# A vision tower on one core: the attention peaks turned into rows by four heads in three parts, in place of six heads in two

## What is computed

```python
qkv = x_qkv.reshape(B, N, 3, NUM_HEADS, HEAD_DIM).transpose(2, 0, 3, 1, 4)
attn = jax.nn.softmax(jnp.einsum('bhqd,bhkd->bhqk', q, k) * scale, axis=-1)
x_attn = jnp.einsum('bhqk,bhkd->bhqd', attn, v)
y2 = jnp.concatenate([x_mlp, x_attn], axis=-1)
```

## Time and profile before

| | us |
|---|---|
| median of 3 runs | 1977.3 |
| lowest, highest | 1976.71, 1978.36 |
| the profiled execution | 1970.27 |
| its span | 1968.5 |

### The profile page before, as it was taken

How to read it: one execution, slowest core, us unless ns; L and a number is a source line. 1 busy time by engine, 2 the same in 40 slices (tenths; PEclk the granted TensorE clock), 3 DMA queues, 4 the chain that set the end, 5 groups by cost and what they waited for, 6 DMA issues and landing times.

```text
span 1968.5 us, 38799 instructions
## 1 busy us (share of the span) xinstructions
PE 1608.9 (82%) x12434; PEld 1287.7 (65%) x12434; DVE 1226.8 (62%) x2822; ACT 845.9 (43%) x1934; POOL 248.9 (13%) x318
## 2 busy tenths in 40 slices
PE   4116289978898799987899789987899788998998
PEld 2004177757686577766777577765787577777786
DVE  2466757684686747685676837776576847563553
ACT  1001065434544345434554345433554346445653
POOL 2002101110022001110021100210011100210000
PEclk8557589978899779987999789987999789999999
DMA  2896646445555435555355446446364442212220
GB/s 72 221 229 163 172 83 143 109 111 132 122 122 113 119 87 137 136 117 136 95 114 134 108 101 149 111 114 159 69 145 116 109 121 50 39 23 41 51 56 15
DMA packets 161084, 218.51 MB, mean 111 GB/s; under 512 B 135099, under 2 KB 149605, under 8 KB 150118
## 3 DMA queue, kind: packets, MB, share of 16 engines
q10 hardware_dynamic: 12288, 154.15, 29.7%
q1 hardware_dynamic: 148582, 61.68, 17.8%
HBM read 186.57 MB, written 28.90 MB: 109 GB/s over the span
## 4 chain that ended last, share of the span: by engine, by line
PE 39%; issue 37%; DMA 9%; DVE 8%; POOL 3%; ACT 2%; SPq 1%; POOLq 0%; DVEq 0%; ACTq 0%
PE bank L952 7%; PE bank L859 7%; DMA xt<-in_x_dram 4%; PE bank L887 4%; PE bank L921 3%; PE bank L869 3%; DMA ks<-qk_scratch 3%; PE bank L906 2%; DVE psums L1211 2%; POOL var L1466 2%; PE bank L767 2%; PE bank L783 2%; DVE peaks L1403 2%; PE bank L734 1%; PE bank L849 1%
## 5 line engine op out<-in xcount | busy, mean ns | idle before, releaser
L1403 DVE TENSOR_REDUCE peaks<-bank 98x2 f32<-98x392 f32 x768 | 425.4, 562 | 318.6 <-PE bank L887 301.3
L1099 ACT ACTIVATE Pb<-bank 98x392 f32<-98x392 f32 x768 | 374.8, 497 | 337.5 <-PE bank L906 285.6
L1211 DVE TENSOR_REDUCE psums<-xt 112x2 f32<-112x512 f32 x672 | 442.6, 679 | 85.1 <-DMA xt<-in_x_dram 52.3
L887 PE MATMUL bank<-ks,qs 96*98 96x196 f16 x1536 | 274.1, 267 | 62.9 <-DVE peaks L1403 40.3
L952 PE MATMUL bank<-w2T,hid 128*98 128x192 f32 x1536 | 306.2, 338 | 0.0
L906 PE MATMUL bank<-qs,ks 97*98 97x196 f16 x1536 | 275.0, 264 | 3.1 <-ACT Pb L1099 2.7
L887 PEld LDWEIGHTS bank<-ks,qs 96*98 96x98 f16 x1536 | 164.8, 130 | 171.7 <-issue 79.5
L952 PEld LDWEIGHTS bank<-w2T,hid 128*98 128x98 f32 x1536 | 244.7, 173 | 2.6
L921 PE MATMUL bank<-Pb,vals 98*32 98x196 f32 x3072 | 186.7, 365 | 5.1 <-DVEq L1397 2.5
L906 PEld LDWEIGHTS bank<-qs,ks 97*98 97x98 f16 x1536 | 173.8, 134 | 17.4 <-issue 9.6
L734 PE MATMUL bank<-spread_p,cst 112*24 112x196 f32 x192 | 49.2, 406 | 127.0 <-POOL spread_p L1457 127.0
(11 more groups left out here) (181 smaller groups left out, 1896.6 us busy)
## 6 DMA issues: line engine op xcount, KB each, us to landing
xt<-in_x_dram ACTq DMA_DIRECT2D x96, 1568.0 KB, 9.1
qk_scratch<-qk SPq DMA_DIRECT2D x64, 294.0 KB, 3.7
qs<-qk_scratch SPq DMA_DIRECT2D x192, 73.5 KB, 3.3
ks<-qk_scratch SPq DMA_DIRECT2D x192, 73.5 KB, 3.6
out_dram<-fin SPq DMA_DIRECT2D x64, 147.0 KB
qs<-shiftT SPq DMA_DIRECT2D x128, 2.3 KB
hid<-in_L_ffn_w_dram SPq DMA_DIRECT2D x1, 1440.0 KB
hid<-in_L_ffn_w_dram SPq DMA_DIRECT2D x1, 960.0 KB
```

Of the source, the lines that this page charges most:

```text
L887: mm = pe.matmul(peak_ps[s][0:HT, T * q:T * q + T], qs[0:KS, i % NSTACK, h, HT * q:HT * q + HT], ks[0:KS, i % NSTACK, h, :], start=True, s ...
L1099: act.activation(Pb[:, (H * i + h) % NP, :, :].rearrange("p a b -> p (a b)"), score_ps[s][0:HT, 0:2 * T], ACT.Exp, scale=float(DH) ** -0.5 ...
L1211: last = dve.tensor_reduce(psums[:, m % 2, t, 2 * p:2 * p + 2], v[:, 2 * p:2 * p + 2, :, :], AX.XY, ALU.add)
L1403: dve.tensor_reduce(peaks[:, h // 6, :, h % 6], peak_ps[s][0:HT, 0:2 * T].rearrange("p (q k) -> p q k", q=2), AX.X, ALU.max, negate=True). ...
```

## The change

The peaks become rows in three parts of four heads (QUAD = 4) in place of two parts of six. `peaks` and `shiftT` have the shapes that go with it, there are three `shift_in` semaphores, and scores wait at heads 0, 4 and 8. Parts 0 and 1 of image i + 1 now follow the mixes in slots 5 and 9 of image i. Part 2 of image i follows the mix in slot 1 of image i itself, so it stands behind that slot's `fill`, which holds `project`. In `opening`, parts 0 and 1 of image 0 come at i = 4 and i = 6; part 2 is in slot 1 of the turn that follows.

```diff
-        if i == 4:
-            ops.append(("shift", dg, 0, 0))
-    ops.append(("shift", dg, 0, 1))
+        if i in (4, 6):
+            ops.append(("shift", dg, 0, i // 2 - 2))
...
         if i:
-            fill[0] = [("shift", 0, i, 1)] + fill[0]
...
         if i + 1 < GRP:
-            fill[7] = [("shift", 0, i + 1, 0)] + fill[7]
             fill[10] = [("values", 0, i + 1)] + fill[10]
...
             ops += fill[h]
             if h in (MIX_LAG, QUAD + MIX_LAG):
                 ops.append(("mix", 0, i, h // QUAD - 1))
-            if i and h == MIX_LAG - 4:
-                ops.append(("mix", 0, i - 1, H // QUAD - 1))
+                if i + 1 < GRP:
+                    ops.append(("shift", 0, i + 1, h // QUAD - 1))
+            if h == MIX_LAG - QUAD:
+                if i:
+                    ops.append(("mix", 0, i - 1, H // QUAD - 1))
+                ops.append(("shift", 0, i, H // QUAD - 1))
...
-        peaks = sb("peaks", [HT, 2, 2, 6])
-        shiftT = sb("shiftT", [6, 2, T], F16)
+        peaks = sb("peaks", [HT, H // QUAD, 2, QUAD])
+        shiftT = sb("shiftT", [QUAD, H // QUAD, T], F16)
...
-                sp.wait_ge(shift_ready, 2 * n_ + part + 1)
-                sp.dma_start(qs[KS:KS + 1, i % NSTACK, 6 * part:6 * part + 6, :],
+                sp.wait_ge(shift_ready, H // QUAD * n_ + part + 1)
+                sp.dma_start(qs[KS:KS + 1, i % NSTACK, QUAD * part:QUAD * part + QUAD, :],
                              shiftT[:, part, :]).then_inc(shift_in[part], 16)
...
-                if h % 6 == 0:
-                    pe.wait_ge(shift_in[h // 6], 16 * (GRP * G_ + i + 1) + ONE)
+                if h % QUAD == 0:
+                    pe.wait_ge(shift_in[h // QUAD], 16 * (GRP * G_ + i + 1) + ONE)
...
-                if h % 6 == 5:
+                if h % QUAD == QUAD - 1:
                     dve.wait_ge(peak_free[s], n_ + ONE)
                     dve.sem_inc(peaks_ready, 1)
```

More of the change, by code:

```diff
@@ L515, in bass_vit_tower @@
         shift_ready = sem("shift_ready")
-        shift_in = [sem(f"shift_in{s}") for s in range(2)]
+        shift_in = [sem(f"shift_in{s}") for s in range(H // QUAD)]
         oT_ready = sem("oT_ready")
@@ L893, in shift @@
                 ps, full = ring(at, "shift", (dg, i, part))
-                pe.wait_ge(peaks_ready, 2 * (GRP * G_ + i) + part + 1)
+                pe.wait_ge(peaks_ready, H // QUAD * (GRP * G_ + i) + part + 1)
                 for q in range(2):
-                    mm = pe.transpose(ps[0:6, HT * q:HT * q + HT], peaks[:, part, q, :], ident[0:HT, 0:HT])
+                    mm = pe.transpose(ps[0:QUAD, HT * q:HT * q + HT], peaks[:, part, q, :], ident[0:HT, 0:HT])
                 mm.then_inc(full, 1)
@@ L1092, in shift @@
                 act.wait_ge(shift_in[part], 16 * n_ + ONE)
-                evac(shiftT[:, part, :], ps[0:6, 0:T], free, shift_ready, 2 * n_ + part + 1)
+                evac(shiftT[:, part, :], ps[0:QUAD, 0:T], free, shift_ready, H // QUAD * n_ + part + 1)
             def score(at, G_, dg, i, h):
@@ L1402, in peak @@
                 dve.wait_ge(peak_full[s], n_)
-                dve.tensor_reduce(peaks[:, h // 6, :, h % 6],
+                dve.tensor_reduce(peaks[:, h // QUAD, :, h % QUAD],
                                   peak_ps[s][0:HT, 0:2 * T].rearrange("p (q k) -> p q k", q=2),
                                   AX.X, ALU.max, negate=True).then_inc(peak_free[s], 1)
-                if h % 6 == 5:
+                if h % QUAD == QUAD - 1:
                     dve.wait_ge(peak_free[s], n_ + ONE)
```

## The result

| | before | after |
|---|---|---|
| median, us | 1977.4 | 2158.0 |
| lowest, highest | 1976.7, 1978.4 | 2153.5, 2161.0 |
| span of the profiled execution | 1968.5 | 2156.6 |
| mean granted clock of PE | 0.871 | 0.843 |

The ratio is 1.091, with a 95% interval of 1.089 to 1.093. The kernel with three parts is 181 us slower. The two profiled executions are 188 us apart, and sums over traces are set against that.

The account below looks back on a forecast made before the run. PE, busy 82% of the span, was taken as the bound. Waits and clock, 24.9 us a turn, gave 149 in six; plus 17 and 8 after the loop, less 2: +172 on 1977.3, called 2150, range 2065 to 2235.

Parts of the forecast that it names:

- SP's queue: Part 2 stands behind project's store and six loads on SP; PE waits at score 8, 19.9 us a turn.
- rival B: At score 8 the part lands on its own, 1.7 us after issue, not with the loads: 2000 us; chance 0.09.
- The sizes of the waits: PE's waits at score 8 in images 0, 1, 2, 3, 5: 2.2, 6.1, 3.2 cut to 0.3, 3.6, 4.8 us.
- The push of the slow clock on the next image: Slow PE behind image 1's wait moves image 2's score 8 some 5 us later, shrinking its wait to about 0.3.
- The clock's whole share: PE at the lower clock behind score 8's waits costs 11.5 us in each of six turns, plus 8 after the loop.
- What the waits give back: New waits overlap later ones: 1.0 us behind image 1, and 2.6 of the 3.13 us at the gate rows behind image 5.
- The 4.48 us wait: PE's wait before image 7's last transpose, once a turn, moves to the chosen tokens' transposes as DVE is late; no gain taken.
- Rival C: The wait before image 7's last part goes and part 2 is free at score 8: about 1927 us; chance 0.05.
- Work and short waits: On PE, 64 added parts cost 10.9 us; 28 mostly short waits at the part's transposes, 13.3 us, go: -2 us.
- The 4 us: For the whole kernel's time, a measurement tells from no change what is over 0.2%, 4 us.

Follow-up runs that it names:

- e1: Three-part kernel with only SP's order changed: part 2's DMA for images 0 to 5 issued right behind project's store, ahead of the six loads; 1985.9 us.
- e2: Three-part kernel with part 2 of images 0 to 5 put ahead of project in slot 1 on all engines; 2000.2 us.
- e5: Three-part kernel with part 2's DMA issued by ACT behind its own copy, in all 64 images, instead of by SP; 1991.6 us.
- e3: Two-part kernel before the change, with the second part moved from slot 0 to behind slot 1's mix and so behind project; 2293.6 us.
- e4: Three-part kernel with 40 unused matmuls on PE ahead of score 8's wait, in images 1, 2 and 5 of the six loop turns; 2129.3 us.
- e6: Two-part kernel before the change, with the second part one slot later, at the head of slot 1, still ahead of project; 1989.7 us.
- e9: Two-part kernel before the change, with 13 unused matmuls on PE ahead of the 4.62 us wait for the planes ending image 7, in six loop turns; 1964.1 us.
- e10: As e9, plus 13 unused matmuls ahead of the wait for image 7's second part and 9 ahead of the gate rows' wait; 1963.1 us.

## Why the prediction came out

It said 2150 us, 2065 to 2235, slower with 0.92; measured were 2158.

**SP's queue.** Right. e1, e2 and e5 take the part from behind the loads, in three ways, and the cost goes; e3 puts two-part work behind them and pays more, with nothing added. e1 changes SP's order alone, so it is the one that leaves no rival for where the part stands.

The third part lands with the loads (3.1 and 8.6 us after its issue), so rival B falls. How much of that is the queue and how much the traffic is shown in part. By the semaphores' updates in the traces (no view prints them), a part lands 1.6 us after its issue in image 7, where nothing is ahead of it, 3.0 to 3.4 us in images 0, 2 and 4, with the loads ahead, and 7.6 to 9.3 us in images 1, 3 and 5, with the loads and an x tile. But an x tile without the loads delays it too: in image 4 of e2 it is issued 1.1 us behind an x tile and ahead of project's store and loads, and it took 6.6 to 7.3 us. It cost nothing there, as it was issued some 9 us ahead of the first load, and PE was not there yet. So in the odd images the order on the queue and the tile were not told apart for the landing; the late issue, behind the wait for the store and six loads, is common to all. The prediction says that the trace of before has no part behind loads with somebody waiting; it had nine directly behind a sixth load with nobody waiting, and by the same updates they landed after 2.3 to 3.5 us, which speaks against B beforehand. The fixed cost of about 2.0 us that the prediction takes from the Trainium skill (DMA: Bandwidth & Descriptors, Anatomy of one DMA) is given there for DMAs issued from GpSimd, and not from SP; here a part with nothing ahead of it took 1.6 us.

**The sizes of the waits**, forecast against measured in one turn: image 0, 2.2 and 1.83; image 1, 6.1 and 5.98; image 2, 0.3 after the clock's help and 3.91; image 3, 3.6 and 1.86; image 5, 4.8 and 4.83. The sum was 17.0, measured 18.4. Over the six turns the means are 1.86, 5.71, 3.84, 2.66 and 4.76, in sum 18.8. There were 39 waits, where some 36 were foreseen, and the largest are in images 1, 5 and 2, not 1, 5 and 3.

**The push of the slow clock on the next image** is the step that failed in its place and its size. It was to shrink image 2's wait from 3.2 to 0.3 us; measured are 3.91 in the turn shown and 3.84 on average. I had a slow stretch of some 10 us behind image 1's wait; it was short, and the long one came behind image 2's:

```profile
1322.60:1329.30 6.70, 3.29 (x14) 2.99 (x15) 0.44 (x1) 0.61 (x2) 0.00 (x0) 0.50 0.33 33
...
1350.00:1366.80 16.80, 15.87 (x78) 12.47 (x82) 8.11 (x16) 5.71 (x13) 2.49 (x5) 0.50 0.04 10
```

The first ends 3.3 us past the 5.98 us wait, the second 16 us past the 3.91 us one. So image 2 had its full wait, and it was image 3's that shrank, by less than foreseen. The six turns bear this out: where the slow stretch ended 3.6 us past image 2's wait (one turn), image 3 waited 3.46 us; where it ended 12.7 to 13.1 us past it (four turns), 2.55 to 2.83; where it ended 16 us past it, 1.86. In e3 image 2's wait did not shrink behind image 1's either (6.1 us, where 5.6 was worked out without a push). The length of a wait does not tell the length of the slow stretch behind it.

**The total is luck in part.** The prediction's sum gave images 0, 1, 2, 3 and 5 of a turn 3.7, 10.1, 0.3, 8.6 and 2.2 us, 24.9 in all. They grew by 3.7, 6.6, 7.5, 5.7 and 3.1, and the turn by 26.7. Images 1 and 3 were 6.4 us too dear, image 2 was 7.2 us too cheap, and the errors cancel. The waits behind the loads and the presence of the clock's price were right; how that price is spread over the images was not.

**The clock's whole share.** From the mean clocks, the time at 0.50 is 2 x (1 - 0.871) x 1968.5 = 508 us before and 2 x (1 - 0.843) x 2156.6 = 677 after. 169 us more at half the pace are some 85 us, where I had 6 x 11.5 + 8 = 77. With the 125 us of waits this is 210; the profiled execution lost 188. The difference was not traced; slow time in which PE stood anyway costs nothing more, and some waits shrank. e4 fits this: its time at 0.50 is 2 x (1 - 0.865) x 2130.4 = 575 us, 102 less than after, which at half the pace is 51; it gained 29 and 15 more went back into waits.

**What the waits give back.** The 3.13 us wait at the gate rows became 1.31, so 1.8 were overlapped and not 2.6; behind it came four waits of 0.7 to 1.1 us for DVE in image 6, which took it back.

**The 4.48 us wait.** As forecast, it stands at the chosen tokens now (3.65 us in the turn shown), and moving the part away from it brought nothing in e6. Rival C falls: images 6 and 7 together are 0.5 us quicker in a turn, and not 4.5 and more.

**Work and short waits.** I set 10.9 us of added work against 13.3 us of short waits, -2 us. One of the 28 was not short (3.06 us, at image 7 of group 6). e1, which has just these two, is 7.5 us above the kernel before, and a turn is 1.3 us longer, the full price of the work. That short waits are a gain is the second step that failed: e6 removes them with no work added and gains nothing. The 4 us that were to tell a change from none are too few: in one set of executions the kernel before took from 1965 to 1992 us.

## To carry to other kernels

Before an entry is moved in a common list, walk each engine's list past the new place, the DMA queues above all: here a transfer of 1.5 KB went behind a wait for a store and six loads that nobody was in a hurry for, and cost 9%. If a part must come late, a place in the queue's own order (between a store and the wait for it), with the other engines' order left as it is, was the cheapest here (e1, 1986 us against 2000 in e2), though not quicker than two parts. Where PE's clock falls in a wait ahead of work that PE bounds, matmuls of no use put into that wait can pay (0.7% in e9); where another engine was late they brought nothing (e10).

## What the runs showed of the hardware beyond what was expected

- A small DMA behind six loads on the same queue landed with them (3.1 and 8.6 us after its issue). One with no load ahead but an x tile under way took 6.6 to 7.3 us (e2, image 4), and one with nothing ahead 1.6 (image 7).
- Loads of 73.5 KB land in 2.7 to 3.7 us beside nothing. Beside an x tile of 1568 KB nearly all take 7.6 to 9.4; with the tiles cut, 87 of 125 us of waits for the part behind them went.
- A wait of 5.98 us was followed by 3.3 us at the lower clock, one of 3.91 us by 16 us, in the same turn, though PE was busy for 15.87 of the 16.80 us of the second stretch. What decides this was not tried.
- In e9 the clock stayed at 1.00 through 4.5 us of matmuls that did nothing, and then fell in the next image 0 in three of six turns, where before it did so in one.
